# Reordering four hand-offs in a two-layer block: layer-norm subtraction, gate softplus, decay exponentials, and the first step of the second expert matrix product

## What is computed

```python
# layer 0
xn = _layernorm(x)
x = x + tile(softmax(q @ k.T, axis=1) @ v, 16) + mixture_of_low_rank_experts(xn)
# layer 1
xn = _layernorm(x)
x = x + gated_linear_attention(xn) + moe(xn)

# gated linear attention (16 heads, 32 key and 64 value channels each)
gk = log_sigmoid(xn @ Wgk1 @ Wgk2 + bgk2) / 16
h = h * exp(gt)[..., None] + kt[..., None] * vt[..., None, :]     # for each token
ot = einsum('bhk,bhkv->bhv', qt * scale, h)
o = o * rsqrt(mean(o * o) + eps) * gnw * silu(xn @ Wg)
return o @ Wo

# moe, 8 experts: every expert is computed for every token
logits = rms_normalised(xn @ gate_w.T + gate_b)
norm_g = top gate / (top gate + 1e-6)
h = gelu(einsum('nd,edh->neh', xf, w1) + b1)
y = einsum('neh,ehd->ned', h, w2) + b2
out = (y * norm_g[:, None, None]).sum(axis=1)
```

## Time and profile before

| | |
|---|---|
| median of the 2 timed runs | 9239.11 us (9177.02 and 9301.21) |
| the profiled execution's own time | 9103.57 us |
| its span on the slowest core (core 1) | 9101.6 us (other cores 9072.1 to 9097.8) |
| outside the span | 2.0 us |
| PE busy, share of the span | 7756.4 us, 85% |
| ACT busy | 3833.6 us, 42% |
| DVE busy | 2590.6 us, 28% |

### The profile page before, as it was taken

How to read it: one execution, slowest core, us unless ns; L and a number is a source line. 1 busy time by engine, 2 the same in 40 slices (tenths; PEclk the granted TensorE clock), 3 DMA queues, 4 the chain that set the end, 5 groups by cost and what they waited for, 6 DMA issues and landing times. The chain is left out here.

```text
span 9101.6 us, 84042 instructions; the slowest of 8 cores (9072.1 to 9101.6 us)
## 1 busy us (share of the span) xinstructions
PE 7756.4 (85%) x31404; PEld 3735.7 (41%) x31404; DVE 2590.6 (28%) x3859; ACT 3833.6 (42%) x3964; POOL 7.5 (0%) x15
## 2 busy tenths in 40 slices
PE   5696769999997679999997778999997777999998
PEld 3363444444443443444443443444443443444443
DVE  2221123333331113333331112333332112333332
ACT  2121016555651105655662014565564003566554
POOL 0000000000000000000000000000000000000000
PEclk7656769999997669999998669999998678999998
DMA  1001202222222112223222112222321121222233
GB/s 51 0 0 65 70 28 93 95 100 88 98 92 80 33 47 92 93 93 100 92 98 69 40 60 79 93 95 93 100 91 58 60 74 60 95 95 98 91 100 102
DMA packets 207022, 696.36 MB, mean 77 GB/s; under 512 B 29088, under 2 KB 30120, under 8 KB 206624
## 3 DMA queue, kind: packets, MB, share of 16 engines
q1 hardware_dynamic: 202048, 673.27, 22.8%
q0 software_dynamic: 4576, 17.71, 0.6%
HBM read 682.51 MB, written 8.39 MB: 76 GB/s over the span
## 5 line engine op out<-in xcount | busy, mean ns | idle before, releaser
L1350 PE MATMUL ps<-XNFH,W1SH 128*128 128x512 bf16 x4096 | 1559.8, 381 | 311.2 <-DVE W1SL L1236 310.7
L1400 PE MATMUL ps<-W2SH,H1FH 128*128 128x512 bf16 x4096 | 1563.3, 382 | 72.5 <-ACT HTMP L1365 72.5
L1403 PE MATMUL ps<-W2SL,H1FH 128*128 128x512 bf16 x4096 | 1564.0, 382 | 0.0
L1410 PE MATMUL ps<-W2SH,H1FL 128*128 128x512 bf16 x4096 | 1563.7, 382 | 0.0
L1354 PE MATMUL ps<-XNFH,W1SL 128*128 128x512 bf16 x4096 | 1559.7, 381 | 0.0
L1352 PE MATMUL ps<-XNFL,W1SH 128*128 128x512 bf16 x4096 | 1559.6, 381 | 0.0
L1249 ACT ACT_TABLE_LOAD x512 | 656.9, 1283 | 1398.0 <-PE ps L1410 1374.1
L1257 DVE TENSOR_TENSOR W2SL<-W2SF,W2SH 128x1024 bf16<-128x1024 f32 x512 | 627.5, 1226 | 1970.2 <-ACT W2SH L1249 1970.2
L1365 ACT ACT_TABLE_LOAD x512 | 656.9, 1283 | 893.6 <-PE ps L1354 892.5
L1236 DVE TENSOR_TENSOR W1SL<-W1SF,W1SH 128x1024 bf16<-128x1024 f32 x512 | 627.5, 1226 | 617.8 <-ACT W1SH L1228 617.8
L1350 PEld LDWEIGHTS ps<-XNFH,W1SH 128*128 128x128 bf16 x4096 | 400.7, 98 | 933.1 <-issue 507.3
(11 more groups left out here) (181 smaller groups left out, 4762.8 us busy)
## 6 DMA issues: line engine op xcount, KB each, us to landing
W1SF<-w SPq DMA_DIRECT2D x512, 512.0 KB, 3.4
W2SF<-w SPq DMA_DIRECT2D x512, 512.0 KB, 3.4
WSLAB<-wv SPq DMA_DIRECT2D x64, 512.0 KB, 4.2
WSLAB<-wg SPq DMA_DIRECT2D x64, 512.0 KB, 3.4
WSLAB<-wo SPq DMA_DIRECT2D x64, 512.0 KB, 3.4
WSLAB<-wq SPq DMA_DIRECT2D x64, 256.0 KB, 2.8
WSLAB<-wk SPq DMA_DIRECT2D x64, 256.0 KB, 2.6
X<-x POOLq DMA_DIRECT2D x1, 8192.0 KB, 29.6
```

Source lines behind the costliest of these rows:

```text
L1350: t.matmul(ps[:, ab: ab + 512], B["W1SH"][:, half + dc * 128: half + dc * 128 + 128], XH[:, dc * 512:(dc + 1) * 512], start=(dc == 0), sto ...
L1400: t.matmul(ps[:, yb: yb + 512], B["H1FH"][:, hsl], B["W2SH"][:, half + dh * 512: half + dh * 512 + 512], start=(hc == 0), stop=False)
L1403: t.matmul(ps[:, yb: yb + 512], B["H1FH"][:, hsl], B["W2SL"][:, half + dh * 512: half + dh * 512 + 512], start=False, stop=False)
L1410: ii = t.matmul(ps[:, yb: yb + 512], B["H1FL"][:, hsl], B["W2SH"][:, half + dh * 512: half + dh * 512 + 512], start=False, stop=(hc == 15))
```

## The change

Four places are edited; what is computed is the same.

- `ln_norm`: the subtraction is a helper `ln_sub`. The one for chunk `ch - 1` is now written behind the normalising of chunk `ch`, and the last one behind the loop. It waits for the ACT copies of its own chunk.
- Decay gate: the bias addition raises `vsem` once per chunk; ACT has one block per chunk, each with `Exp`, `drain`, `Ln` and an increment. PE's L972 for chunk 0 waits for chunk 0's `Ln` alone. Since `c.ss` is no longer what PE waits for there, the count of the last `DECS` is kept in `c.decs_last`, and the wait is for the larger of the two.
- `front`: a `drain` between `EB` and `ENB` on ACT, and one between `QTL` and `KTL` on DVE, are gone.
- Experts, phase B, step 0: the chunks are taken in the order 3, 0, 1, 2, and the wait for the last `Gelu` stands ahead of chunk 2.

```diff
+            def ln_sub(ch, po):
+                @blk.vector
+                def _(v, ch=ch, po=po):
+                    v.wait_ge(ssem, c.lncp[ch % 2])
+                    for dcb in range(8):
...
+                        ii = v.tensor_tensor(XNFL[:, co], pso, XNFH[:, co], ALU.subtract)
+                    ii.then_inc(vsem, 1)
+                    c.vs += 1
...
+                if hilo and ch > 0:
+                    ln_sub(ch - 1, 3072 if (ch - 1) % 2 else 0)
...
-                if hilo:
-                    @blk.vector
-                    def _(v, ch=ch, po=po):
-                        v.wait_ge(ssem, c.ss)
...
+            if hilo:
+                ln_sub(3, 3072)
...
         for ch in range(2):
-            ii = v.tensor_tensor(B["EXN"][:, ch * 512:(ch + 1) * 512],
-                                 ps[:, ch * 512:(ch + 1) * 512], B["BGK2T"][:],
-                                 ALU.add)
-        ii.then_inc(vsem, 1)
-        c.vs += 1
-
-    @blk.scalar
-    def _(s):
-        s.wait_ge(vsem, c.vs)
-        for ch in range(2):
+            v.tensor_tensor(B["EXN"][:, ch * 512:(ch + 1) * 512],
+                            ps[:, ch * 512:(ch + 1) * 512], B["BGK2T"][:],
+                            ALU.add).then_inc(vsem, 1)
+            c.vs += 1
+
+    for ch in range(2):
+        @blk.scalar
+        def _(s, ch=ch):
+            s.wait_ge(vsem, c.vs - 1 + ch)
             s.activation(B["EXN"][:, ch * 512:(ch + 1) * 512],
                          B["EXN"][:, ch * 512:(ch + 1) * 512], AF.Exp, scale=-1.0)
-        s.drain()
-        for ch in range(2):
-            ii = s.activation(B["SPT"][:, ch * 512:(ch + 1) * 512],
-                              B["EXN"][:, ch * 512:(ch + 1) * 512], AF.Ln, bias=1.0)
-        ii.then_inc(ssem, 1)
-        c.ss += 1
+            s.drain()
+            s.activation(B["SPT"][:, ch * 512:(ch + 1) * 512],
+                         B["EXN"][:, ch * 512:(ch + 1) * 512], AF.Ln,
+                         bias=1.0).then_inc(ssem, 1)
+            c.ss += 1
+        spt_ss.append(c.ss)
...
-            t.wait_ge(ssem, c.ss)
+            t.wait_ge(ssem, max(spt_ss[ch], c.decs_last))
...
             s.activation(B["EB"][:], ps[:, 2560:3072], AF.Exp, scale=-1.0 / 16)
-            s.drain()
             s.activation(B["ENB"][:], ps[:, 2560:3072], AF.Exp, scale=1.0 / 16).then_inc(ssem, 1)
...
-            v.drain()
             v.tensor_tensor(B["KTL"][:], B["KT"][:, ch * 512:(ch + 1) * 512], B["ENB"][:],
...
-                if hc == 0:
-                    t.wait_ge(ssem, ss0 + 16)
                 half = (hc % 2) * 1024
-                for tc in (2, 3, 0, 1):
+                for tc in ((3, 0, 1, 2) if hc == 0 else (2, 3, 0, 1)):
+                    if hc == 0 and tc == 2:
+                        t.wait_ge(ssem, ss0 + 16)
```

More of the change, by code:

```diff
@@ L82, in __init__ @@
         self.rsv = 0
+        self.decs_last = 0
         self.wsl = [0] * 8
@@ L256, in ln_norm @@
         def ln_norm(blk, tt, hilo=False):
+            def ln_sub(ch, po):
[3 more added lines that the diff above has]
+                    for dcb in range(8):
+                        co = slice(dcb * 512 + ch * 128, dcb * 512 + ch * 128 + 128)
+                        pso = ps[:, po + dcb * 128: po + dcb * 128 + 128]
+                        ii = v.tensor_tensor(XNFL[:, co], pso, XNFH[:, co], ALU.subtract)
+                    ii.then_inc(vsem, 1)
+                    c.vs += 1
             for ch in range(4):
@@ L938, in _ @@
         c.ts += 1
+    spt_ss = []
     @blk.vector
@@ L1079, in _ @@
             c.ss += 1
+        c.decs_last = c.ss
         @blk.vector
```

## The result

Over twelve runs the changed kernel has a median of 9270.12 us (8931.19 to 9831.95); before, run beside it, has 9588.49 us over ten (9160.41 to 10080.22). The runs that were not disturbed (in the others the cores of one die show a lower granted clock) compare as 0.9745, 95% interval 0.9722 to 0.9769. The two profiled executions took 9103.57 and 8932.18 us, ratio 0.9812. So the change is worth 1.8 to 2.6%, and the traces account for 1.9 to 2.0.

A forecast was written before the change was run, and what follows sets the result against it. No engine bounds the whole: PE bounds the experts, chains of small pieces the rest. Gains 56 + 77 + 13 + 11 + 5 = 162 us, taken from the 9239 us median, give 9077 us, range 8950 to 9160.

The forecast's parts named there:

- the terms' ends: Low and high bounds of the priced gains: about 70 to 191 us, giving 9048 to 9169 us.
- two of the rivals, 9167 and 9259: Border wait returns inside phase B, 9167 us, chance 0.08; late slabs make each expert wait again, 9259 us, chance 0.02.
- Layer norm: Normalising ahead of the gate matmuls: later subtraction hides behind ACT's copying, 14.0 us less a tile, 56 us in four.
- The rival that ACT and DVE hinder each other at PSUM: Layer norm gains nothing as both engines get in each other's way: 106 us gain, 9133 us, chance 0.07.
- Border: Phase A to phase B in the experts: PE's wait for the last `Gelu` hides, 32 x 2.42 = 77 us.
- Clock: Behind the borders: falls of the granted clock, 1.7 us each, 15 us together, of which 13 us counted as gain.
- Decay gate and drains: Attention: `EB` 1.39 us earlier in eight halves, 11 us; two drains removed, 16 x 0.33 = 5 us.
- The rival "the clock gives more back": Experts: clock falls elsewhere go too, other terms at upper bounds; gain 191 us, 9048 us, chance 0.24.
- The one that ends slower: Experts, phase A: late slabs make each expert wait once more, costing 182 us; 9259 us, chance 0.02.

The follow-up runs named there:

- `a_best2`: `a_best` with the first two W2 splits one step later in phase A; 8607.22 us, before on the same chip 9102.30.
- `p_gate`: The kernel before with only the decay gate split by chunk, drains kept; 9097.45 us, before on that chip 9105.00.
- `a_oneblock`: The changed kernel with the decay gate of both chunks in one block of ACT; 9004.91 us.
- `p_border`: The kernel before with only the new chunk order and later `Gelu` wait in phase B, step 0; 9008.28 and 9008.89 us, before 9105.00.
- `p_ln`: The kernel before with only the later layer-norm subtraction; 9041.30 and 9043.11 us, before on that chip 9105.00.
- `a_best`: `a_oneblock` with `Gelu` and the following W1 cast of phase A also in one block of ACT; 8730.58 us.
- `a_best_again`: `a_best` unedited, run again on the chip of `a_best2`; 8674.11, 8681.96 and 8689.70 us.

## Why the prediction was right and wrong

*The median, and with it the range, was wrong.* The step that failed is the last one, "the forecast is 9239 - 162 = 9077 us" with a range of 8950 to 9160. It took the median of two runs as the level, and held that other runs could only move it down. The measured median is 9270.12, outside the range, although the gain was larger than forecast, because before itself came to 9588.49 over ten runs, 349 us above the level that I built on. Eight of those ten lie above 9300 us and two at 9160 and 9177; of the twelve of the changed kernel eight lie above 9070 and four at 8931 to 8944. So each median is one of the long runs, and how long those are is not in the price of any wait. The two runs shown were 1.4% apart and both over the profiled one; that was a hint that such a median has no meaning to 1%. The range had a fault of its own: its upper end of 9160 lies below the 9169 that the terms' ends give and below two of the rivals, 9167 and 9259. Differences against the profiled execution, or ratios, hold; absolute medians here do not.

*The sign and the mechanism were right, and the size of the gain nearly.* Forecast 162 us, 1.8%; the profiles give 171 (slowest core) and 181 (mean), 1.9 to 2.0%; the comparisons 1.85% and 2.55%, one on each side of the 2% on which the chances turned.

- Layer norm: 56 forecast, 55 to 56 measured, the chain to 0.1 us (22.4 and 22.33 a tile). The rival that ACT and DVE hinder each other at PSUM is out: 1.68 us for the subtraction as before.
- Border: 77 forecast, 77.6 measured, in two kernels. Reading the lost time from starts (2.42) and not from the idle time in the row (2.26) was worth 5 us of that.
- Clock: 13 forecast, 16.5 measured for the falls behind the borders. Their number was right (9 on core 1, 9.9 in the mean), and so was the price of one, 1.7 us, here and in `a_best2`; 10 of before's 121 falls last 6.8 us instead of 3.4. The 2 us taken off for falls that stay did not come to that: phase A lost 18 us to half clock before and 19 after, 8 of them at the starts of the tiles. What the forecast did not have is the half clock in the last steps of the tiles (6.7 us less) and 7 us less by starts of waits in phase A; neither is shown to be the change's.
- Decay gate and drains: 11 and 5 forecast, 1.37 x 8 = 11 and 5 by the timelines, 14 together in the stage. The Trainium skill's figure for a change of set ("ScalarE: Activation LUTs", "What ACT_TABLE_LOAD costs") would have left nothing of the 11. `p_gate` shows 1.28 for a load and `Exp` 0.01 us behind it; but in `a_oneblock` `Exp` and `Ln` run from one load, so the added load is no change of set, and this case does not test that figure.
- The rival "the clock gives more back" came nearest in the size of the gain (181 of 191 us), but not by its mechanism: falls elsewhere in the experts did not get fewer (5.0 a core before, 5.9 after, 8.0 in `p_border`). The one that ends slower did not occur: with the border gone PE waits in phase A as before (258 and 265 us).

## What to carry to other kernels

Read what a wait of TensorE costs from the starts of the matmuls on both sides of it and from the clock behind it, and first remove the few long waits: here 32 of 2.4 us a program were worth 94 us with the clock, while some 230 shorter ones, of about 0.9 us in their rows, cost 1.08 us each and no clock. Where a wait guards one bank, do first what touches the others. Code that is split into more blocks of ScalarE brings a table load with each; before removing a load, look what it hides. A forecast of a time, and not of a difference, needs a level that more than two runs have shown.

## What the hardware showed that I had not expected

- The short falls of the granted clock came with waits of PE of about 2 us or more and not with waits of 0.88 us, however many: all 492 falls in the profiles of before, the changed kernel, `p_ln`, `p_border`, `a_best` and `a_best_again` have a wait of 1.90 us or more in the 8 us ahead of them. Not every such wait brings one (at the borders 9.9 of 32). Without long waits the experts have no such fall in 5366 us (`a_best2`), on any of eight cores.
- Half clock came without any wait too: in the last step of a tile's experts, where float32 matmuls with one row stand among the bfloat16 ones, in 18 (`a_best2`) to 28 (before) of 32 cases, for up to 92 us, on into the next tile.
- A fall cost 1.7 us, half of the 3.4 us that it lasts, in before as in `a_best_again`.
- Chips differ by stage: on one of them the float32 matmuls of attention run with stretches of 0.81 (0.94 in the window of projections shown), and attention takes 52 us more an execution, while the bfloat16 experts take the same time there (5686 and 5681 us).
- Two functions, `Gelu` and the cast of a copy, run from one table load when they stand in one block: the loads ahead of the W1 casts went from 512 to 64 in `a_best`.
